# The bias of the norm behind the attention, made by GpSimd in two products instead of by VectorE in one

## What is computed

```python
x = x + _L0_xattn_ref(ctx_1024, _layernorm(x), L0_xattn_wq, L0_xattn_wk, L0_xattn_wv)
x = x + _L0_attn_ref(_layernorm(x), ...)      # this norm: (x - mean) / sqrt(var + 1e-5), then the scan
x = x + _L0_ffn_ref(_layernorm(x), ...)
x = x + _L1_xattn_ref(_layernorm(x), ctx_1024, ctx_1024, ...)   # its keys are made in the first loop too
x = x + _L1_attn_ref(_layernorm(x), ...)
x = x + _L1_ffn_ref(_layernorm(x), ...)
```

## Time and profile before

| what | value |
|---|---|
| median of 3 runs | 1841.49 us (1839.72 to 1842.4) |
| profiled execution | 1841.54 us, span 1839.7 us |
| PE, busy share of the span | 90% |
| DVE, busy share of the span | 83% |
| ACT, busy share of the span | 81% |
| POOL, busy share of the span | 65% |
| mean granted TensorE clock | 0.947 |

### The profile page before, as it was taken

The page is one execution under the profiler, slowest core; times in us unless marked ns, Lnnn a source line. Parts: engine busy times, 40 slices in busy tenths (PEclk is TensorE's granted clock), DMA queues, the critical chain, the costliest instruction groups (busy, mean ns, idle before and its releaser), DMA issues. The chain is left out here.

```text
span 1839.7 us, 41845 instructions
## 1 busy us (share of the span) xinstructions
PE 1657.3 (90%) x14000; PEld 1139.7 (62%) x14031; DVE 1535.6 (83%) x2803; ACT 1496.0 (81%) x3463; POOL 1189.9 (65%) x1365
## 2 busy tenths in 40 slices
PE   7999999999999999999999863579999999999974
PEld 4665566565565666566565531457777777777752
DVE  5449999999999999999999898637788888888853
ACT  4579998999999999989989978126788888888864
POOL 2446667667676676666766654148788878888752
PEclk9999999999999999999999986779999999999976
DMA  9413122122121221222222130000000000000000
GB/s 254 139 53 115 52 91 89 52 98 81 61 104 67 99 80 53 104 75 63 93 64 81 46 109 2 18 9 8 17 14 17 14 14 14 15 16 14 11 8 12
DMA packets 54227, 107.13 MB, mean 58 GB/s; under 512 B 8400, under 2 KB 30928, under 8 KB 49232
## 3 DMA queue, kind: packets, MB, share of 16 engines
q1 hardware_dynamic: 54096, 105.51, 17.6%
HBM read 96.97 MB, written 8.52 MB: 57 GB/s over the span
## 5 line engine op out<-in xcount | busy, mean ns | idle before, releaser
L762 ACT ACTIVATE abuf<-delta,cols 128x496 f32<-128x496 f32 x512 | 330.8, 702 | 5.5 <-DVE yac L1019 3.1
L932 POOL TENSOR_TENSOR yac<-yac,gP 128x1024 f32<-128x1024 f32 x128 | 302.3, 2361 | 37.6 <-ACT gP L771 36.6
L1019 DVE TENSOR_TENSOR_SCAN gP<-abuf,ps_s 128x512 f32<-128x512 f32 x256 | 296.2, 1199 | 0.4 <-POOL yac L932 0.4
L580 PE MATMUL ps_kv<-w_k,cT 128*128 128x256 f32 x1024 | 255.3, 392 | 0.0
L592 PE MATMUL ps_kv<-kcube,cx 128*128 128x256 f32 x1024 | 253.7, 392 | 0.6 <-ACT kcube L802 0.5
L592 PEld LDWEIGHTS ps_kv<-kcube,cx 128*128 128x128 f32 x1024 | 195.2, 195 | 64.0 <-issue 34.5
L922 POOL TENSOR_TENSOR kcube<-kcube,ksq 128x512 f32<-128x512 f32 x128 | 165.7, 1295 | 91.1 <-ACT ksq L784 90.9
L652 PE MATMUL ps_kv<-hT,w_pT 128*128 128x512 f32 x384 | 189.8, 618 | 31.4 <-ACT delta L847 24.3
L580 PEld LDWEIGHTS ps_kv<-w_k,cT 128*128 128x128 f32 x1024 | 184.2, 190 | 48.7 <-issue 29.1
L771 ACT ACTIVATE gP<-gP,cols 128x512 f32<-128x512 f32 x256 | 169.9, 715 | 0.0
L912 POOL TENSOR_TENSOR rat<-s,roots 128x8 f32<-128x8 f32 x64 | 105.9, 1654 | 93.7 <-ACT junk L791 93.7
(11 more groups left out here) (324 smaller groups left out, 4106.4 us busy)
## 6 DMA issues: line engine op xcount, KB each, us to landing
cT<-in_h_ctxT SPq DMA_DIRECT2D x32, 1028.0 KB, 7.4
cx<-in_ctx SPq DMA_DIRECT2D x32, 1024.0 KB, 5.5
xT<-in_h_xT SPq DMA_DIRECT2D x8, 512.0 KB, 3.7
xcur<-in_x SPq DMA_DIRECT2D x32, 128.0 KB, 2.0
left_n<-in_ctx SPq DMA_DIRECT2D x128, 32.0 KB, 1.8
x_mid<-xb SPq DMA_DIRECT2D x16, 256.0 KB, 2.6
x_c<-x_mid SPq DMA_DIRECT2D x32, 128.0 KB, 2.0
out<-y SPq DMA_DIRECT2D x32, 128.0 KB, 1.7
```

What stands on the lines that cost most here:

```text
L580: last = pe.matmul(bank[:, j * D:(j + 1) * D], cT[G % 2][:, b, dc, j * P:(j + 1) * P], w_k[:, dc, :], start=False, stop=(dc == DC - 1), sk ...
L762: act.activation(abuf[q % 2][:, i, :].rearrange("p (b t) -> p b t", t=T)[:, :, 1:T], delta[J % 2][:, :].rearrange("p (b t) -> p b t", t=T) ...
L932: pool.tensor_tensor(yac[:, :, :], yac[:, :, :], pool_home(q)[:, :, :], ALU.add).then_inc(S["pacc_done"], 1)
L1019: dve.tensor_tensor_scan(dst[:, i, :], abuf[q % 2][:, i, :], ps_u[:, :], 0.0, ALU.mult, ALU.add).then_inc(S["scan_done"], 1)
```

## The change

DVE no longer makes `nbias`. POOL makes it in two tensor_tensor products of 128 x 1: `mean * -1` ahead of the pow (a column of `nhalf` now holds -1.0 instead of -0.5), and that times `rstd1` behind it. The pow and the first product raise `x_rstd` together to 2A + 2, and POOL waits for that before its second product. The wait that kept `nbias` from being overwritten before ACT had read it (`lnh_ready`) goes to POOL too, and DVE gets a wait on `nbias_ready` of the group before, ahead of the bn_aggr that overwrites `mv1`.

```diff
         @block.gpsimd
         def _(pool):
-            pool.memset(nhalf[:, :], -0.5)
+            pool.memset(nhalf[:, 0:1], -0.5)
+            pool.memset(nhalf[:, 1:2], -1.0)
...
         if A is not None:
             pool.wait_ge(S["x_var"], A + 1)
+            if A:
+                pool.wait_ge(S["lnh_ready"], A)
+            pool.tensor_tensor(nbias[:, :], mv1[:, 0:1], nhalf[:, 1:2], ALU.mult).then_inc(S["x_rstd"], 1)
             pool.tensor_tensor(rstd1[:, :], ve1[:, :], nhalf[:, 0:1], ALU.pow).then_inc(S["x_rstd"], 1)
+            pool.wait_ge(S["x_rstd"], 2 * A + 2)
+            pool.tensor_tensor(nbias[:, :], nbias[:, :], rstd1[:, :], ALU.mult).then_inc(S["nbias_ready"], 1)
         if J is not None:
             pool_add(pool, J, 2)
...
             apart(dve)
+            if A:
+                dve.wait_ge(S["nbias_ready"], A)
             dve.bn_aggr(mv1[:, :], bst[:, :]).then_inc(S["x_bst"], 1)
...
             dve.tensor_copy(kse[:, :], ps_f[:, D:2 * D]).then_inc(S["kse_ready"], 1)
-        if A is not None:
-            dve.wait_ge(S["x_rstd"], A + 1)
-            if A:
-                dve.wait_ge(S["lnh_ready"], A)
-            dve.scalar_tensor_tensor(out=nbias[:, :], in0=mv1[:, 0:1], scalar=-1.0, in1=rstd1[:, :], op0=ALU.mult,
-                                     op1=ALU.mult).then_inc(S["nbias_ready"], 1)
         if g == 0 and 2 <= sc <= NS:
             dve_out(dve, sc - 2, 0)
```

More of the change, by code:

```diff
@@ L132 @@
 ENDED = tuple((n, NG) for n in (
-    "xb_ready x0_bst x0_var x0_rstd x_var x_rstd nbias_ready lnh_ready hT_full hT_ready s_full negm_ready p_ready pT_full "
+    "xb_ready x0_bst x0_var x0_rstd x_var nbias_ready lnh_ready hT_full hT_ready s_full negm_ready p_ready pT_full "
     "pT_ready pv_full o_ready oT_full oT_ready o_full x_added fin_full kse_full kse_ready kst_full kvt_ready kv_half kv_added "
     "ks_added y_read y_summed yg_ready").split()) + tuple((n, B) for n in (
-        "k_full kf_ready s2_ready k3_ready s6_ready kn_ready g_full gs_ready").split()) + (("x_bst", 2 * NG), ("mx_ready", 2 * NG),
+        "k_full kf_ready s2_ready k3_ready s6_ready kn_ready g_full gs_ready").split()) + (("x_bst", 2 * NG), ("x_rstd", 2 * NG), ("mx_ready", 2 * NG),
     ("rinv_ready", NG), ("y_state", NACC * NG), ("scan_done", NST * NG), ("decay_ready", NST * NG), ("y_full", NPE * NG))
```

## The result

The changed kernel took 1807.61 us, median of 4 runs (1806.52 to 1809.82), against 1840.61 us for four of before: 33.0 us less, ratio 0.9821 with a 95% interval of 0.9804 to 0.9838. Run again later beside the experiments it took 1805.08 us against 1842.06, ratio 0.9802 (0.9786 to 0.9819).

The account below looks back on a forecast made before the run. It took PE, DVE and ACT as all nearly full, ACT tightest. 16 DVE-led steps at 1.05 us (16.8) plus 3.6 us made 20.4, rounded to 20: 1841.5 - 20 = 1821.5 us, range 1807 to 1833.

Parts of the forecast that it names:

- The stall and its size: DVE's nbias line L1185 waits about 1.84 us per instance beside POOL's add; 16 DVE-led steps, 29.4 us.
- The scan doesn't inherit it: DVE's next instruction, scan L1019 with one SBUF and one PSUM input, stays at 1185 to 1221 ns.
- POOL's added time: The two products and a wait on POOL add 0.55 us per step, between 0.3 and 1.35 us.
- What ACT lets through: ACT is tightest: its idle time for the fourth key block gives back only about 1.4 us per leading step.
- POOL's delay: POOL's later cube of key block 2 makes ACT's L791 late by about 0.37 us.
- 0.6 per four on top: PE carries part of its gain into steps it leads: 0.6 us for each of 6 fours, 3.6 us.
- PE's cap of 33.1 us: PE can give back only its waits at L683 for DVE, so the gain is at most 33.1 us.
- rival A: ACT lets more through, so DVE's gain counts whole: 29.4 up to 33.1 us, 1808 to 1812 us; chance 0.17.
- the sum: 16 leading steps at 1.05 us, 16.8 us, plus 3.6 us: 20.4, rounded to 20 us gained.
- Rival B: The stall moves to another two-input DVE line, L1142 or L1131: only 9 us gained, 1832.5 us; chance 0.14.
- C: The scan behind L1185 is held by POOL's add instead: 2.2 us count, 1839 us; chance 0.06.
- D: POOL's tiny products cost 1.66 us each, making ACT late: 30 us lost, 1872 us; chance 0.05.

Follow-up runs that it names:

- e1: Kernel before, with nbias still made on DVE but by a tensor_scalar with one input tensor and a per-partition scalar column: 1802.2 us, ratio 0.9789.
- e3: Kernel before, with only POOL's order changed, the cube of key block 2 ahead of the add of scan pair 2: 1818.03 us, ratio 0.9865.
- e5: Changed kernel plus DVE's old two-input instruction into a spare column, waiting for POOL's second product: 1847.9 us, ratio 1.0037.
- e7: Changed kernel plus a second making of the normed rows on ACT, 0.49 us per step: 1810.74 us, ratio 0.9835.
- e10: Kernel before plus a second making of the normed rows on ACT, 0.49 us per step: 1839.95 us, ratio 0.9998.
- e11: The same edit of the kernel before as e1, run again: 1802.41 us, ratio 0.9792.
- e12: e1's edit, with the first half of the kv_all addition also moved behind the sum that waits for POOL's join: 1800.32 us, ratio 0.979.
- e2: Changed kernel plus DVE's old two-input instruction into a spare column, at its old place behind x_rstd: 1806.76 us, ratio 0.9811.

## Why the prediction was right or wrong, point by point

**The stall and its size: right.** 1.84 us of each blocked instance was waiting for POOL's add, and it was on the path of the steps that DVE led: the first of four got 1.92 us shorter. e1, e3 and e5 show it from three sides.

**The scan doesn't inherit it: right.** 248 scans into `gP` between 100 and 1100 us, with one SBUF input each:

```profile
L1025 DVE TENSOR_TENSOR_SCAN gP<-abuf,ps_s x248: 1186/1197/1222, 130.7 to 1083.1; 128x512 f32<-128x512 f32 x124
```

**POOL's added time: a little less than forecast.** From the start of the chain to the add it is 584.36 - 583.39 = 0.97 us, against 605.83 - 605.26 = 0.57: 0.40 us instead of 0.55. The products took 0.23 and 0.19, and the pow 0.56 instead of 0.60. `rstd0` moved forward as worked out: it runs at once behind the cube.

**"What ACT lets through": a step that failed.** I wrote that ACT is the tightest and lets about 1.4 us per leading step through, less 0.37 for POOL's delay, 1.05 in all, with 0.6 per four on top: 2.7 us per four steps. 4.55 came. The first leading step of a four gained 1.92, more than ACT was to let through. The waits of ACT, 300 to 900 us, before, and after:

```profile
ACT ksq L784 <- DVE kcube L1046: 22.5, 15, 2.2
ACT delta L847 <- PE ps_kv L652: 8.4, 9, 1.4
ACT Gs L810 <- PE ps_kv L592: 4.7, 4, 1.3
ACT qT L816 <- PE ps_kv L554: 3.9, 7, 1.0
ACT dx L860 <- issue: 2.4, 9, 0.5
```

```profile
ACT delta L848 <- PE ps_kv L653: 5.7, 4, 1.4
ACT ksq L785 <- DVE kcube L1052: 5.2, 4, 1.3
ACT Gs L811 <- PE ps_kv L593: 5.1, 4, 1.3
ACT hT L826 <- PE ps_m L684: 2.5, 4, 0.6
ACT junk L792 <- POOL kcube L923: 1.5, 5, 0.4
ACT dx L861 <- issue: 1.0, 4, 0.2
ACT qT L817 <- PE ps_kv L555: 0.9, 5, 0.2
```

Before, 41.9 us in 600 / 133.2 = 4.5 fours are 9.3 us of waiting per four; after, 21.9 us in 4.66 fours are 4.7. ACT gave 4.6 us per four, as much as the period shrank by, and still has as much again. (An engine whose work stays the same always waits less by what the period shrinks; the rows say that it could, e7 and e10 that it didn't lead.) I had counted one wait, that for the key block, in the two steps only; the waits for `delta`, `dx` and `qT` were spare time of the same engine in the same four and went too. And POOL's delay met ACT in 5 of some 19 steps with 1.5 us in all, not 0.37 in each leading one. e10 shows it on the kernel before: 0.49 us more on ACT in each step cost nothing there.

**PE's cap of 33.1 us: no cap, and the clock was left out.** PE's waits at L683, worth 35.7 us, are gone but for 3.0, as rival A had it, whose price was 29.4 to 33.1. That 33.0 were gained is chance, though: the 28 steps gained 34.2, and e1 and e11, which only take the stall away, gained 40.3 and 38.5 in their medians. The cap counted PE's waits and put its clock at nothing. The eight low stretches cost PE 8 x 1.7 = 13.7 us, of which an estimated 9 to 14 (8 x 1.1 to 8 x 1.7) were in the time of the steps. In return PE waits somewhat more elsewhere, at L629 for DVE's copy 8.1 us instead of 3.5.

**Why the sum came so near.** Put together from the steps of before that have no low clock (31.27, 31.86, 32.51 and 35.95 us), four steps would have taken 131.6 us: 3.0 more than the changed kernel's 128.6, where 2.7 were forecast. That is luck, as ACT was not what limited them. The other 1.6 of the 4.55 us are, by this estimate, the clock's.

**Rival B happened, and cost nothing that can be seen.** Not at L1142 but at the first half of the `kv_all` addition, which I had not priced. By line, 100 to 1100 us, and timelines of DVE and of POOL:

```profile
L1131 DVE SCALAR_TENSOR_TENSOR kv_all<-kvt,pairmask,kv_all x30: 344/796/906, 123.3 to 1044.4; 128x128 f32<-128x128 f32 x30
...
L1148 DVE SCALAR_TENSOR_TENSOR yg<-gate,yg x31: 666/681/684, 157.8 to 1098.6; 128x512 f32<-128x512 f32 x31
...
600.69 0.88 DVE L1131 SCALAR_TENSOR_TENSOR kv_all<-kvt,pairmask,kv_all 128x128 f32<-128x128 f32 x1
...
600.15 1.27 POOL L938 TENSOR_TENSOR yac<-yac 128x512 f32<-128x512 f32 x1
```

It ends 0.15 us behind the join (601.57 and 601.42), and the next line waits for that join anyway; e12 removed it, and the steps got no shorter. The line took 20.4 us in these 30 instances instead of 11.3 before, which is 9 of the 14 us by which DVE's busy time fell less than forecast (31 instead of 45); the other 5 stay open.

**Rivals C and D** are out by the rows of the scans and of POOL's products.

**What stays open.** PE leads the fourth step of each four. No single engine leads the other three: in the 28 steps about half of what PE gets counts, a quarter of 0.49 us on ACT (3.5 of 13.7 us) and about half of 0.43 on POOL (6.5 of 12.0). Why the low clock followed on one of the two waits of a four and not on the other isn't shown.

## What to carry to other kernels

Look at the mean time of instructions that should be tiny: a 128 x 1 line of 2 us is a wait that the profile records as work. Where a DVE instruction with two SBUF inputs meets long GpSimd instructions, first give it a per-partition scalar operand (e1) or one PSUM input (as the scans have); moving it to GpSimd took the stall away too, but cost 3.5 us here. When several engines are nearly full, what one of them can give back is bounded by the sum of all its waits over a whole period, not by the one wait that stands opposite the edit; a run with a little more work on that engine, on the kernel before, measures it directly. A wait of the matmul engine can cost more than its own length: look at the granted clock behind it, in windows of a few microseconds, as an average over 200 us (0.99 against 1.00 here) hides it. And where medians scatter by as much as the effect, the same two points of a periodic timeline can tell a few tenths of a microsecond per period.

## What the runs showed of the hardware that was not expected

Who comes first is decided within a few hundredths of a microsecond: recorded 0.01 or 0.02 us behind the start of POOL's add the line took 0.14 us (e2, 20 times), once 0.03 us behind it 2.35 us (e2), and 0.08 us behind it 2.30 us (e5). Behind eight of PE's waits of 2.05 to 2.41 us the granted clock fell to 0.50 for 3.4 us; in the changed kernel, where no such wait stands between 100 and 1000 us, it didn't fall there. A per-partition scalar column read from SBUF beside one input tensor did not wait for POOL (192 to 214 ns, 32 times, e1). POOL's product of one column takes 0.19 to 0.23 us and its pow of one column 0.56, its pow of eight 1.66.
